# A routed-expert block on one core: a reordered turn, super groups 3,4,3,2,2,2, and eight unread products ahead of each projection

## What is computed

```python
mod = (silu(c) @ wmod)                      # six vectors of 128 for each sequence
h = layernorm(x) * (1 + ca) + sa
g, a = sigmoid(h @ Wg.T + bg), sigmoid(h @ Wd.T + bd)
v = h @ Wv.T + bv
s_t = a_t * s_(t-1) + (1 - a_t) * v_t        # a scan over the 256 tokens of a sequence
x = x + ga * (s * g)
h = layernorm(x) * (1 + cb) + sb
probs = softmax(h @ gate_w.T + gate_b)       # 8 experts, the 2 best of each token are kept
y_e = relu(h @ w1[e] + b1[e]) @ w2[e] + b2[e]
out = x + gb * sum over the 2 best of probs_e * y_e
```

## Time and profile before

| What | Value |
|---|---|
| median of three runs | 541.35 us |
| the profiled execution's own time | 545.22 us |
| its span, first to last instruction | 543.4 us |
| busy: PE, DVE, ACT, POOL | 424.1, 448.6, 308.7, 210.1 us |
| mean granted clock of TensorE | 0.878 |
| 64 scatters `sorted_rows` L521 on POOL | 68.0 us busy, mean 1062 ns |
| 96 instructions of `project`, L1121 | 64.7 us busy |

### The profile page before, as it was taken

One profiled execution on the slowest core, in us unless ns is written; L12 is line 12 of the kernel. 1 busy time (PEld: TensorE's weight loads), 2 busy tenths in 40 slices (PEclk: granted clock), 3 DMA queues, 4 the chain that ended last, 5 costly groups with the idle time before them and its releaser, 6 DMA issues.

```text
span 543.4 us, 14857 instructions
## 1 busy us (share of the span) xinstructions
PE 424.1 (78%) x4290; PEld 348.0 (64%) x4291; DVE 448.6 (83%) x1242; ACT 308.7 (57%) x777; POOL 210.1 (39%) x279
## 2 busy tenths in 40 slices
PE   2837898784875861069999999999999999999970
PEld 2423655552643751049988998898897888888860
DVE  5799869854798868369999999999999888989960
ACT  1427989773866430046666666656665555556630
POOL 5003322237667357702433443344334433333331
PEclk9868889786979555569999999999999999999985
DMA  8413444114233224231332233223323322222210
GB/s 240 117 39 123 154 140 141 68 46 180 100 117 147 90 99 153 102 88 38 97 94 76 76 99 87 73 77 96 88 79 77 87 80 73 76 67 75 64 37 0
DMA packets 46567, 51.01 MB, mean 94 GB/s; under 512 B 5422, under 2 KB 39679, under 8 KB 46514
## 3 DMA queue, kind: packets, MB, share of 16 engines
q1 hardware_dynamic: 38400, 33.17, 22.1%
q0 software_dynamic: 7040, 16.93, 8.4%
q10 hardware_dynamic: 1074, 0.23, 0.2%
HBM read 27.43 MB, written 24.70 MB: 96 GB/s over the span
## 4 chain that ended last, share of the span: by engine, by line
PE 40%; issue 19%; DVE 19%; POOL 13%; ACT 3%; DMA 2%; SPq 1%; POOLq 0%; DVEq 0%; ACTq 0%
POOL sorted_rows L521 12%; PE bank L1241 5%; PE bank L1257 5%; PE bank L1258 5%; PE bank L1260 5%; PE bank L1243 5%; PE bank L1242 5%; DVE xs L1038 4%; PE bank L1121 4%; DVE st L763 2%; PE bank L1253 2%; DVE hT L1051 2%; PE bank L1227 2%; DVE xn L809 1%; DVE a L1056 1%
## 5 line engine op out<-in xcount | busy, mean ns | idle before, releaser
L542 POOL DMA_INDIRECT out_dram<-tg,midx x92 | 106.7, 1159 | 198.7 <-DVE tg L1059 184.7
L705 ACT ACTIVATE xs<-bank,bcols 128x256 f32<-128x256 f32 x368 | 139.4, 489 | 32.4 <-PE bank L1243 32.0
L1257 PE MATMUL bank<-w2hi,xs 128*128 x736 | 122.7, 220 | 0.0
L1258 PE MATMUL bank<-w2hi,w2f 128*128 x736 | 122.6, 220 | 0.0
L1040 DVE TENSOR_TENSOR w2f<-xs 128x1024 f16<-128x1024 f32 x92 | 112.7, 1225 | 3.2
L1260 PE MATMUL bank<-w2lo,xs 128*128 x736 | 101.7, 220 | 0.0
L1241 PE MATMUL bank<-xh,w1hi 128*128 128x256 f16 x368 | 101.4, 276 | 0.3 <-ACT xs L705 0.3
L1242 PE MATMUL bank<-xl,w1hi 128*128 128x256 f16 x368 | 101.3, 275 | 0.0
L1243 PE MATMUL bank<-xh,w1lo 128*128 128x256 f16 x368 | 101.2, 275 | 0.0
L521 POOL DMA_INDIRECT sorted_rows<-pay,idx x64 | 68.0, 1062 | 34.5 <-issue 18.9
L1258 PEld LDWEIGHTS bank<-w2hi,w2f 128*128 128x128 f16 x736 | 72.5, 99 | 0.0
(11 more groups left out here) (221 smaller groups left out, 706.4 us busy)
## 6 DMA issues: line engine op xcount, KB each, us to landing
xs<-sorted_rows SPq DMA_DIRECT2D x46, 260.0 KB, 2.8
xs<-sorted_rows SPq DMA_DIRECT2D x47, 128.0 KB, 2.5
sorted_rows<-padt SPq DMA_DIRECT2D x10, 582.0 KB, 5.2
w2f<-in_L_ffn_w_dram SPq DMA_DIRECT2D x4, 512.0 KB, 3.8
xs<-in_L_ffn_w_dram SPq DMA_DIRECT2D x4, 512.0 KB, 4.0
out_dram<-tg,midx POOLq DMA_INDIRECT x92, 3.1
xs<-in_L_attn_x_dram SPq DMA_DIRECT2D x2, 512.0 KB, 7.5
sorted_rows<-pay,idx POOLq DMA_INDIRECT x64, 2.7
```

What stands on the lines that cost most here:

```text
L542: pool.indirect_dma_start(out_rows, bass.IndirectOffsetOnAxis(midx[k][:, t:t + 1], 0), yout[k][:, t, :], None, bounds_check=TOK - 1, oob_i ...
L705: ins = act.activation(hf[e][:, cc, :], bank[2 * e + cc // 2][:, (cc % 2) * TW:(cc % 2 + 1) * TW], ACT.Relu, bias=bcols[n % 2][:, e * HC + ...
L1257: pe.matmul(o[t], hh[n % 2][e][:, cc, t * P:(t + 1) * P], whi, start=False, stop=False)
L1258: pe.matmul(o[t], hl[n % 2][e][:, cc, t * P:(t + 1) * P], whi, start=False, stop=False)
```

## The change

1. `SGS` is 3,4,3,2,2,2. `CHOOSE_IN`, `PAIR_IN` and `PLACE_IN` of the first two super groups come one turn earlier, but for the placing of the second, which stays in turn 12. `X_CHUNKS` loads groups 0 and 1 singly, then 2 and 3, 4 and 5; the first is issued ahead of wmod. Batch 2 of the variances is no longer finished on DVE but on POOL.
2. DVE: in each turn `residual` and `variances` come ahead of `choose`, `pair_rows` and `place_rows`. Normalizing of group 3 comes behind residual 0. In the first two batches the statistics of a further group are written between the dependent steps.
3. PE: `turn_r` comes right behind `project`; `spread_gb` of the turn's own group closes the turn. ACT: `copy_gb` of the turn's own group comes behind `payload`.
4. PE runs 8 bf16 products of a 128x128 matrix of ones with 512 columns of ones ahead of the first transpose and ahead of each projection of turns 0 to 14, into bank 2, where nothing reads them.

```diff
-SGS = (4, 4, 2, 2, 2, 2)
+SGS = (3, 4, 3, 2, 2, 2)
-X_CHUNKS = ((0, 1), (2, 3, 4, 5), (6, 7, 8, 9), (10, 11, 12, 13), (14, 15))
+X_CHUNKS = ((0,), (1,), (2, 3), (4, 5), (6, 7, 8, 9), (10, 11, 12, 13), (14, 15))
-QUICK = (0, 1, 2) + tuple(range(len(BATCHES) - 4, len(BATCHES)))
+QUICK = (0, 1) + tuple(range(len(BATCHES) - 4, len(BATCHES)))
-CHOOSE_IN = {7: 0, 11: 1, 13: 2, 14: 3}
-PAIR_IN = {8: 0, 12: 1, 13: 2, 15: 3}
-PLACE_IN = {9: 0, 12: 1, 14: 2}
+CHOOSE_IN = {6: 0, 10: 1, 13: 2, 14: 3}
+PAIR_IN = {7: 0, 11: 1, 13: 2, 15: 3}
+PLACE_IN = {8: 0, 12: 1, 14: 2}
+START_BUSY = 8
+TURN_BUSY = 8
...
             for turn in range(NG):           # ACT
-                if turn >= 1:
-                    copy_gb(turn - 1)
...
                 for g in MOD2_IN[turn]:
                     payload(g)
+                copy_gb(turn)
...
             for g in range(NG):              # DVE
                 scan(g)
                 if g == 0:
-                    stats1(3, 4, 5)
+                    stats1(4, 5)
                     variances(2)
-                if g + 3 < NG:
+                if 0 < g < NG - 3:
                     normalize(g + 3)
...
+                if g == NG - 1:
+                    pair_rows(NSG - 3)
+                residual(g)
+                if g == 0:
+                    normalize(3)
+                for n, (end, _, _) in enumerate(BATCHES):
+                    if end == g > 0:
+                        variances(n)
                 if g in CHOOSE_IN and g < NG - 2:
                     choose(CHOOSE_IN[g])
-                if g in PAIR_IN:
+                if g in PAIR_IN and g < NG - 1:
                     pair_rows(PAIR_IN[g])
                 if g in PLACE_IN:
                     place_rows(PLACE_IN[g])
-                residual(g)
...
+            def keep_busy(o, n):             # PE
+                for _ in range(n):
+                    pe.matmul(o, ones_bf[:, :], ones_bf[:, :].unsqueeze(1).to_broadcast([P, GT, P]), start=True, stop=True)
...
             for turn in range(NG):
-                if turn == 1:
-                    pe.wait_ge(setup_dve, DVE_GBROW)
-                    pe.wait_ge(iota_done, 1)
-                if turn >= 1:
-                    spread_gb(turn - 1)
                 if turn + 1 < NG:
+                    after(pe, z_used, 3 * turn + 1)
+                    keep_busy(bank[2][:, :], TURN_BUSY)
                     project(turn + 1)
+                turn_r(turn)
+                if turn in PLACE_IN and turn not in PAIR_IN:
+                    rank_rows(PLACE_IN[turn])
                 for g in MOD2_IN[turn]:
                     turn_xn2(g)
                 if turn + 2 < NG:
                     turn_xn(turn + 2)
-                turn_r(turn)
-                if turn in PLACE_IN and turn not in PAIR_IN:
-                    rank_rows(PLACE_IN[turn])
                 for g in MOD2_IN[turn]:
                     logits(g)
                     turn_back(g)
+                if turn == 0:
+                    pe.wait_ge(setup_dve, DVE_GBROW)
+                    pe.wait_ge(iota_done, 1)
+                spread_gb(turn)
```

More of the change, by code:

```diff
@@ L241, in adaln_moe_kernel @@
         w1_in, w2_in = ([sem(f"{n}_in{k}") for k in range(4)] for n in ("w1", "w2"))
-        ident_done, iota_done = sem("ident_done"), sem("iota_done")
+        ident_done, ones_done, iota_done = sem("ident_done"), sem("ones_done"), sem("iota_done")
         dve_step, act_step, pool_step = sem("dve_step"), sem("act_step"), sem("pool_step")
@@ L364, in _ @@
             sp.dma_start(csb[:], c).then_inc(csb_in, 16)
+            load_x_chunk(0)
             sp.dma_start(wmods[:], wmod).then_inc(wmod_in, 16)
-            for c_ in range(len(X_CHUNKS)):
+            for c_ in range(1, len(X_CHUNKS)):
                 load_x_chunk(c_)
@@ L457, in _ @@
                                     pattern=[[-1, P]], channel_multiplier=1))
-            for t in (ones16, ones_bf, onesf, upper):
+            pool.memset(ones_bf[:, :], 1.0).then_inc(ones_done, 1)
+            for t in (ones16, onesf, upper):
                 mark(pool.memset(t[:, :], 1.0))
@@ L686, in _ @@
             normalize2(NG - 1)
-            copy_gb(NG - 1)
             modulate2(NG - 1)
@@ L763, in stats, with variances, step @@
                     mark(dve.bn_stats(st[:, first + t, :], row(t)))
-            def variances(n):
+            def variances(n, meanwhile=None):
+                rows = [] if meanwhile is None else list(range(meanwhile * GT, (meanwhile + 1) * GT))
+                def step(ins):
+                    mark(ins)
+                    count = steps
+                    if rows:
+                        t = rows.pop(0)
+                        mark(dve.bn_stats(st[:, t, :], xrow(t)))
+                    dve.wait_ge(dve_step, count)
                 m0, M0, m1, M1 = (batch_cols(st, n)[..., i] for i in (1, 2, 4, 5))
@@ L924, in _ @@
             stats1(0)
-            variances(0)
+            dve.wait_ge(x_in[1], 16)
+            variances(0, meanwhile=1)
             normalize(0)
@@ L931, in _ @@
             dve.tensor_scalar(ca1[:, :], bank[7][:, B:2 * B], 1.0, None, ALU.add).then_inc(setup_dve, 1)
-            stats1(1, 2)
+            stats1(2)
             dve.wait_ge(b_in, 16 * 3)
@@ L938, in _ @@
             dve.tensor_scalar(gabv[:, :], gaN[:, :], bcol[:, 2:3], None, ALU.mult).then_inc(setup_dve, 1)
-            variances(1)
+            variances(1, meanwhile=3)
             normalize(1)
@@ L970, in _ @@
                     place_rows(PLACE_IN[g])
-                residual(g)
-                for n, (end, _, _) in enumerate(BATCHES):
-                    if end == g > 0:
-                        variances(n)
                 if g == NG - 2:
@@ L1096, in turn_xn @@
                 ins.then_inc(xnT_ready, 1)
+            def keep_busy(o, n):
+                for _ in range(n):
+                    pe.matmul(o, ones_bf[:, :], ones_bf[:, :].unsqueeze(1).to_broadcast([P, GT, P]), start=True, stop=True)
             pe.wait_ge(ident_done, 1)
+            pe.wait_ge(ones_done, 1)
+            keep_busy(bank[2][:, :], START_BUSY)
             pe.wait_ge(setup_dve, DVE_CSILU)
@@ L1207, in _ @@
             rank_rows(NSG - 3)
-            spread_gb(NG - 1)
             turn_xn2(NG - 1)
```

## The result

| | before | after |
|---|---|---|
| median (lowest to highest) | 541.3 us (538.31 to 546.0) | 553.22 us (550.71 to 558.61) |
| profiled execution, its own time | 545.22 us | 558.61 us |
| its span | 543.4 us | 556.8 us |
| busy PE, DVE, ACT, POOL | 424.1, 448.6, 308.7, 210.1 us | 454.7, 446.1, 309.3, 213.5 us |
| mean granted clock | 0.878 | 0.869 |

The change costs 2.1%: the ratio is 1.0209 [1.0149, 1.0269], against a forecast of no change. The profiled execution is the slowest of the four and has the lowest granted clock of them (0.869; the others 0.880 to 0.893), so its trace shows the loss at its largest: its own time stands 5.4 us above the median, where the profiled execution before stood 3.9 above. The last scatter is 13.8 us later and the span 13.4 us longer: as the prediction had it, the expert loop did not change, and everything happened ahead of it.

What follows compares the result with a forecast made beforehand. The start of the expert loop was taken as the bound, set by idx 3 plus fixed scatters. The terms summed to -0.2 us, 545.0 us profiled, and with the median 3.9 lower 541 us; range of 8 in 10: 530 to 553.

Steps and rivals of the forecast that it cites:

- The chain and the scatters: The expert loop starts when POOL's scatters end: idx of super group 3 plus a fixed 34.3 us of scatters.
- The start: Up to residual 2: batch 2 leaves DVE, products cost some; residual 2 at 48.0 from 50.42, 2.4 us gained.
- Eight products and the reordered turn: Residual 2 to 12: products add 1.7 us a turn, choosing and placing are hidden; light turn 8.9, sum 88.6 us.
- The clock: Residual 2 to 12: one or two drops to the lower level (1.2 GHz), 2.2 us each on average, 3.4 us taken.
- rival B: Turns 3 to 12: ring hangs on PE, eight drops cost 17.6 us instead of 3.4; 555 us, chance 0.14.
- rival A: Clock holds: no drop in ten turns, 3.4 us less, and PE's end chain about 4 us shorter; 534 us, chance 0.22.
- Idx 1: On DVE, idx of super group 1 comes 7.8 us behind residual 12, at 147.8; before 151.0.
- The ring slot: DVE's wait for a payload slot: 9.64 us in turn 10 goes, 3.9 us at residual 13 is new.
- From idx 1 to idx 2: On DVE, 21.55 us as before, plus 0.8 for more tiles and 3.9 of slot wait; idx 2 at 174.1.
- Idx 2 to idx 3: 4.8 us to r of group 15, 12.3 as before, 2.5 more; idx 3 at 193.7, against 193.89.
- C: Turns: the ring is DVE's or ACT's, PE runs the products while it waits, turn 7.3 us; 525 us, chance 0.13.
- D: DVE's work behind residual delays r, PE waits 1 to 2 us in each of six turns; 550 us, chance 0.06.

Runs made afterwards that it cites:

- e1: The changed kernel without the eight products ahead of each projection (those ahead of the first transpose stay): 538.48 us, ratio 0.9900.
- e4: The changed kernel with four more products in turns 3 to 14 that have logits, between last transpose and logits: 543.49 us, ratio 1.0004.
- e3: The changed kernel with `choose(2)` ahead of residual 13 instead of behind it: 549.98 us, ratio 1.0102.
- e7: The changed kernel with the old super groups 4,4,2,2,2,2 and their old tables of turns: 561.71 us, ratio 1.0338.
- e6: e5 with `choose(2)` ahead of residual 13: 531.12 us, ratio 0.9772.
- e5: The changed kernel with no products ahead of the projections and four between last transpose and logits instead: 536.15 us, ratio 0.9873.
- f1: e6 once more, on one chip beside f2 and f3: 531.99 us, ratio 0.9791.
- f2: f1 with 24 more products in PE's waits of the last turns, same chip: 529.81 us, ratio 0.9749.
- e10: The kernel before, old order and groups, with four products between last transpose and logits only: 551.92 us, ratio 0.9926 on a chip slower than the others.
- e9: e6 with more products in PE's waits of the last turns (same kernel as f2), on the slower chip: 548.71 us, ratio 0.9856.
- e11: e6 with `place_rows(1)` ahead of residual 12 and its ranking written ahead of `turn_r(12)`, on the slower chip: 540.68 us, ratio 0.9706.
- f3: The same kernel as e11, on the chip of f1 and f2: 532.02 us, ratio 0.9795.

## Why the prediction was wrong

**The chain and the scatters: right.** Idx 3 plus a fixed time of scatters held: 33.3 us in the changed kernel (208.24 to 241.51), against 33.8 before (193.89 to 227.67). Nothing behind it changed.

**The start: right in sum** (48.46 for 48.0), with larger terms on both sides. Residual 0 came 4.1 us earlier (30.79 for 34.94), and residual 2 only 2.0. Of the 2.2 us given back e1 puts 1.0 on the products and leaves 1.2 that come without them; the prediction had one term for all. No run divides the 4.1 us among the moved batch, the loads and the order. The batch that moved took 4.2 us on POOL (28.75 to 32.91) for the 4.7 assumed, with every operation at 0.20 to 0.26 us; the longer batch that the prediction allowed for did not come. It does show in the next batch: there the four operations from 43.16 on took 0.53 to 0.67 us beside DVE's scan (42.98 to 45.70), and the same ones 0.22 to 0.32 behind it.

**Eight products and the reordered turn: right in size, in part by luck.** 1.90 us by their busy time at the upper level and 1.73 from their start to the projection's (1.7 forecast), up to 3.6 at the lower; a light turn 8.85 us for 8.9; ten turns without drops 87.5 us (e4) for 88.6. But the 0.3 us credited to the place of copy_gb did not come: two projections without a drop are 7.41 us apart in e1 (65.81 and 73.22) and 7.42 in the kernel before (77.46 and 84.88). And then the products added 1.4 us to such a turn, not 1.7. The two errors cancel.

**The clock: this step failed.** The prediction took "one or two drops in ten turns". There were eight. By e4 they cost 102.3 - 87.5 = 14.8 us, 1.85 each where 2.2 was assumed; the forecast had 3.4 us for all. The traces of e3 and e7, with the same products, have seven and six. That is rival B as written, "drops stay, in a ring that now hangs on PE", with a chance of 0.14. That its time of 555 came so close (553.22) is partly luck: B had the drops alone for 14 us more, and they were 11.4; the rest is the next failed step. I gave it so little for "with 4.4 us of dense work a turn instead of 2.7, the level should return sooner". It did return, within the turn; but it also fell again at the end of the gap or just behind it, and what lay there paid. The sentence "the products make each turn's work longer but not the gap shorter" was the one to go by. It does not explain everything: e1 has the gap and no products, and four drops. Why the eight products bring eight stays open. The rule that rival A cited from the Trainium skill ("TensorE: Matmul & The Clock Gate", the HAM clock gate), that activity releases the throttle, does not by itself tell these runs: from residual 2 to residual 12 eight products more in each turn went with 0.85, below the 0.90 of e1 without any, and four more in the gap brought 1.00.

**Idx 1: right** (7.4 us behind residual 12 for 7.8). The ring slot too: no wait in turn 10, and 4.42 us at residual 13 for 3.9. By e7 the new super groups are worth 7 us by the ratios, and 4.4 us at the last scatter.

**From idx 1 to idx 2: this step failed, by 4.1 us** (30.4 for 26.3). "The same pieces lie between them in the new order" counted DVE's pieces and not who waits for them. `choose(2)` had moved behind residual 13, its slot wait and its dependent steps, PE's logits wait for `choose(2)`, and products and projection stand behind the logits. e3 takes 5.3 us off by moving that one call, and 2.8 us in e6 against e5 (27.9 to 25.1).

**Idx 2 to idx 3: right** (19.7 for 19.6), and at least 4.4 us of it are the lower level (f1, f2), about the 4 us that rival A allowed for it.

Rivals C and D fell: products are not free (e4 against e5, 5.8 us in ten turns even at the upper level), and DVE does not hold PE in the light turns, though it does in turn 8, which is none (below). C had a grain of truth, though. Eight products in each of ten turns would make 17 us at the upper level. Between e5 and e4 there are 5.8, and 9.6 if the 3.8 us are added by which turn 12 of e5, with its drop, is longer than e4's. The rest lies beside DVE's work: where DVE chooses and places, in turns 7 to 9, the turns take 8.1, 9.6 and 8.7 us without the eight and 8.9, 9.6 and 9.3 with them.

The sum, as far as idx 3: drops 11.4 us (14.8 for 3.4), the start 0.5, ten turns without drops -1.1, idx 1 -0.4, the bank 4.1, the tail 0.1: 14.6 us, and idx 3 came 14.5 late (208.24 for 193.7). 541 + 14.5 is 555.5, and the median was 553.22; the profiled execution stood further above the median than the 3.9 us that the forecast took off.

## What to carry to other kernels

Work that is there only to hold a clock belongs in the wait or the stretch of small operations after which the level falls, not ahead of the work that sets the pace: here twelve products a turn, four of them in the gap, cost 11 us less than eight without these. It has to be weighed against none at all, too: eight ahead of the projection lost 17 us against none (e1), and what four in the gap gain over none is small, 0.7% in the old order on one chip (e10) and in the new order too little to be told from e1. And when a step is moved behind a wait on one engine, look for every bank that the step still has to free: another engine may be standing there with its whole turn behind it. The lowest median measured is that of f2, with the change's order and super groups, no products ahead of the projection, four in the gap, `choose(2)` early and products in the last turns: 529.81 us, 2.5% below the kernel before and 4.5% below the changed one by their ratios (0.9749 and 1.0209). On the chip of e9 the same kernel was 1.4% below the kernel before (0.9856).

## What the runs showed of the hardware

- In the changed kernel's trace a drop came in eight of the ten turns 3 to 12, at 1.85 us each by e4, and in four of them the small products just ahead still ran at the upper level (gb 0.71 us). Without the eight products there were four (e1, clock 0.90 for 0.85). With the gap filled none came in the same ten turns (e4, clock 1.00).
- Four small operations on POOL took 0.53 to 0.67 us beside DVE's scan and 0.22 to 0.32 behind it (changed kernel, 43.16 to 47.1 us).
- One chip ran the kernel before in 557.19 us (13 runs), 2.5% above the 543.4 to 544.0 of the three others that the experiments used. Medians of different chips can't be set against each other at the level of the effects here. Ratios are better but not safe either: two kernels measured on that chip and on another gave 0.9856 and 0.9749 (e9, f2), and 0.9706 and 0.9795 (e11, f3), so that even their order turned round. e9's and f2's traces agree up to idx 1 (136.22 and 136.65 us); idx 3 is then 15.5 us later in e9 (192.86 for 177.34), and why is not shown.
